# Moving the row normalisation to ScalarE and rewriting the step-size series in a ViT + Mamba + MoE kernel

## The reference, cut to what matters

```python
x = _patch_embed(images, ...)                 # 197 tokens of 128 features per image
x = _block(x, ...); x = _block(x, ...)        # 8 heads of attention, then a gated feed-forward
h = rmsnorm(x, ln_f)
...
dt = jax.nn.softplus(dt_in @ W_dt + b_dt)     # the step size of the Mamba scan, both directions
dA = jnp.exp(dt[..., None] * A)               # 16 states
dBx = dt[..., None] * Bm[:, :, None, :] * xs[..., None]
...
h = _layernorm(h + mamba_f + mamba_b)         # (x - m) / sqrt(v + eps): the "normalised rows"
h = _layernorm(h + moe(h))
```

## Time and profile before

| what | value |
|---|---|
| median of 3 runs | 8827.63 us (8824.43 to 8831.17) |
| the profiled execution's own time | 8837.69 us |
| its span, first to last instruction | 8835.9 us |
| PE, DVE, ACT busy | 80%, 80%, 70% of the span |
| POOL busy, DMA engines | 9%, about 32% |
| DVE, ACT instructions | 9195, 13424 |
| granted TensorE clock, mean | 0.918 of full speed |

### The profile page before, as it was taken

The page is one execution under the profiler, slowest core; times in us unless marked ns, Lnnn a source line. Parts: engine busy times, 40 slices in busy tenths (PEclk is TensorE's granted clock), DMA queues, the critical chain, the costliest instruction groups (busy, mean ns, idle before and its releaser), DMA issues. The chain is left out here.

```text
span 8835.9 us, 117469 instructions
## 1 busy us (share of the span) xinstructions
PE 7084.8 (80%) x33290; PEld 3962.2 (45%) x33290; DVE 7040.5 (80%) x9195; ACT 6165.8 (70%) x13424; POOL 808.2 (9%) x554
## 2 busy tenths in 40 slices
PE   6777777888888888888888888888888888888661
PEld 3444444444444444444444444444444444444330
DVE  2788888888888888888888888888888888888743
ACT  5766666677777777777777777777777777777434
POOL 0134242400000000000000000000000000000065
PEclk9998888999999999999999999999999999999775
DMA  2333323233333333333333333333333333333356
GB/s 96 110 129 115 116 100 107 102 113 118 117 118 112 117 117 116 112 121 119 118 113 116 116 118 113 117 113 120 113 116 116 117 116 116 114 120 109 129 113 199
DMA packets 282498, 1034.03 MB, mean 117 GB/s; under 512 B 37570, under 2 KB 129526, under 8 KB 273824
## 3 DMA queue, kind: packets, MB, share of 16 engines
q1 hardware_dynamic: 248352, 1009.77, 32.1%
q0 software_dynamic: 33792, 21.18, 1.5%
HBM read 951.57 MB, written 90.94 MB: 118 GB/s over the span
## 5 line engine op out<-in xcount | busy, mean ns | idle before, releaser
L1047 PE MATMUL psS<-KM,Q 128*99 128x394 f32 x4096 | 1712.5, 542 | 310.1 <-ACT PTs L578 227.6
L572 ACT ACTIVATE P<-psS,least_s 99x197 f32<-99x197 f32 x4096 | 1417.3, 434 | 640.7 <-DVE least_s L768 633.0
L843 DVE TENSOR_TENSOR_SCAN hs<-dA,hs 128x1576 f32<-128x1576 f32 x512 | 1762.1, 3442 | 62.2
L768 DVE TENSOR_REDUCE least_s<-psS 99x2 f32<-99x394 f32 x2048 | 1083.7, 560 | 312.1 <-PE psS L1047 290.2
L1054 PE MATMUL psS<-cst,P 99*99 99x99 f32 x8192 | 1077.1, 273 | 255.7 <-ACT P L572 238.6
L1054 PEld LDWEIGHTS psS<-cst,P 99*99 99x99 f32 x8192 | 931.5, 180 | 763.5 <-ACT P L572 588.2
L649 ACT ACTIVATE dA<-dt_,aneg 128x394 f32<-128x394 f32 x2048 | 1211.1, 631 | 28.2 <-DVE hs L843 19.2
L1047 PEld LDWEIGHTS psS<-KM,Q 128*99 128x99 f32 x4096 | 643.2, 178 | 1027.6 <-ACT PTs L578 501.7
L578 ACT ACTIVATE PTs<-psS 99x396 f32<-99x396 f32 x2048 | 969.0, 521 | 104.3 <-PE psS L1054 102.6
L1139 PE MATMUL psY<-hs,cst 128*128 128x394 f32 x2048 | 858.9, 551 | 136.1 <-DVE hs L852 136.1
L829 DVE TENSOR_TENSOR hs<-hs,u 128x1576 f32<-128x1576 f32 x512 | 916.3, 1790 | 52.4 <-DMA hs<-bc_scratch 52.4
(11 more groups left out here) (214 smaller groups left out, 9524.4 us busy)
## 6 DMA issues: line engine op xcount, KB each, us to landing
hs<-bc_scratch SPq DMA_DIRECT2D x512, 788.0 KB, 4.2
cr<-bc_scratch SPq DMA_DIRECT2D x512, 788.0 KB, 5.1
pat<-patches SPq DMA_DIRECT2D x64, 1176.0 KB, 7.6
more_scratch<-zeros SPq DMA_DIRECT2D x64, 197.0 KB, 5.2
rows_scratch<-hs SPq DMA_DIRECT2D x1, 12352.0 KB, 43.7
PTs<-more_scratch SPq DMA_DIRECT2D x24, 512.0 KB, 6.5
sum_scratch<-HW SPq DMA_DIRECT2D x64, 148.5 KB
hs<-rows_scratch SPq DMA_DIRECT2D x24, 386.0 KB, 3.4
```

The lines of the kernel that those rows point to most:

```text
L572: last = nc.scalar.activation(P[:, r, b, m, 0:T], psS[0:CT, 2 * r + b, m * T:(m + 1) * T], ACT.Exp, bias=least_s[:, r, b, m:m + 1], scale= ...
L768: nc.vector.tensor_reduce(least_s[:, r, b, :], psS[0:CT, 2 * r + b, 0:2 * T].rearrange("p (e t) -> p e t", e=2), axis=AX, op=ALU.min).then ...
L843: nc.vector.tensor_tensor_scan(h, a, h, 0.0, ALU.mult, ALU.add).then_inc(scan_ready, 1)
L1047: mm(psS[0:CT, 2 * r + b, 0:2 * T].rearrange("p (e t) -> p e t", e=2), Q[:, r, b, q * CT:(q + 1) * CT], KM[:, r, h % 2 * 2:h % 2 * 2 + 2, ...
```

## The change

It does four things.

1. On ACT, L639 becomes `Square` with `scale = 1/sqrt(3)` and a per-partition `bias = -sqrt(3)/4`: this gives `e^2/3 - e/2 + 3/16`. DVE adds 13/16 and multiplies by `e` in one `scalar_tensor_tensor`. The plain product of L815 is gone.
2. DVE no longer writes the rows. It forms `mrs = -mean * rstd` (99x4), and ACT writes four chunks of 99x128 as `Identity(rstd * x + mrs)` from PSUM. The waits for `rows_stored` and `slots_free` move to ACT too.
3. A constant column is added to `epsr` by POOL at the start, so `pool_ready` counts to 14. The marker semaphore `q_waited`, for which nobody waits, becomes an alias of `pool_waited`.
4. `STAGES` and `PLACE` are replaced.

```diff
-ACT_FRONT, ACT_BACK, DVE_BACK, DVE_ROUTE = (4, 5), 2, 6, 27
+ACT_FRONT, ACT_BACK, DVE_BACK, DVE_ROUTE = (4, 5), 2, 4, 27
...
-        epsr = sb("epsr", [128, 2])
+        epsr = sb("epsr", [128, 3])
...
+        mrs = sb("mrs", [CT, NC4])
...
+            nc.gpsimd.memset(epsr[:, 2:3], -(3 ** 0.5) / 4).then_inc(pool_ready, 1)
...
-                nc.scalar.activation(u[:, d, :], sp[:, :], ACT.Copy, bias=-0.5, scale=1 / 3).then_inc(poly_ready, 1)
+                nc.scalar.activation(u[:, d, :], sp[:, :], ACT.Square, bias=epsr[:, 2:3], scale=3 ** -0.5).then_inc(poly_ready, 1)
...
                 nc.scalar.activation(rstd[:, :], rstd[:, :], ACT.Exp, scale=-0.5).then_inc(rstd_ready, 1)
+                act.wait_ge(mrs_ready, i + 1)
+                act.wait_ge(rstd_ready, i + 1)
+                act.wait_ge(rows_stored, i * 32 + 16)
+                act.wait_ge(slots_free, i + 1)
+                for q in range(NC4):
+                    last = nc.scalar.activation(HW[:, q, 0:D], psY[0:CT, q * D:(q + 1) * D], ACT.Identity, bias=mrs[:, q:q + 1], scale=rstd[:, q:q + 1])
+                last.then_inc(ht_ready, 1)
...
                 dve.wait_ge(poly_ready, k)
-                back(nc.vector.tensor_tensor(u[:, d, :], u[:, d, :], sp[:, :], ALU.mult), i)
+                back(nc.vector.scalar_tensor_tensor(out=u[:, d, :], in0=u[:, d, :], scalar=13 / 16, in1=sp[:, :], op0=ALU.add, op1=ALU.mult), i)
                 dve.wait_ge(sp_ready, k)
-                back(nc.vector.scalar_tensor_tensor(out=u[:, d, :], in0=u[:, d, :], scalar=1.0, in1=sp[:, :], op0=ALU.add, op1=ALU.mult), i)
...
                 dve.wait_ge(rstd_ready, i + 1)
-                dve.wait_ge(rows_stored, i * 32 + 16)
-                dve.wait_ge(slots_free, i + 1)
-                for q in range(NC4):
-                    last = nc.vector.tensor_scalar(HW[:, q, 0:D], tokens[:, q, :], mv[:, q, 0:1], rstd[:, q:q + 1], ALU.subtract, ALU.mult)
-                last.then_inc(ht_ready, 1)
+                nc.vector.scalar_tensor_tensor(out=mrs[:, :], in0=mv[:, :, 0], scalar=-1.0, in1=rstd[:, :], op0=ALU.mult, op1=ALU.mult).then_inc(mrs_ready, 1)
```

More of the change, by code:

```diff
@@ L82, in role_stages @@
     return out
-STAGES = [('square', 1, 0), ('norm', 1, 0), ('conv', 0), ('square', 0, 0), ('qkv', 1), ('keys', 1, 0), ('norm', 0, 0), ('score', 1, 0, 0), ('score', 1, 0, 1), ('qkv', 0), ('keys', 0, 0), ('keys', 1, 1), ('turn', 1, 0, 0), ('turn', 1, 0, 1), ('score', 0, 0, 0), ('score', 1, 1, 0), ('score', 1, 1, 1), ('score', 0, 0, 1), ('turn', 1, 1, 0), ('keys', 0, 1), ('turn', 0, 0, 0), ('turn', 0, 0, 1), ('turn', 1, 1, 1), ('score', 0, 1, 0), ('score', 0, 1, 1), ('score', 1, 2, 0), ('turn', 0, 1, 0), ('score', 1, 2, 1), ('turn', 0, 1, 1), ('keys', 1, 2), ('score', 0, 2, 0), ('score', 0, 2, 1), ('turn', 1, 2, 0), ('turn', 1, 2, 1), ('keys', 0, 2), ('turn', 0, 2, 0), ('turn', 0, 2, 1), ('score', 1, 3, 0), ('score', 1, 3, 1), ('score', 0, 3, 0), ('score', 0, 3, 1), ('keys', 0, 3), ('turn', 0, 3, 0), ('turn', 0, 3, 1), ('keys', 1, 3), ('turn', 1, 3, 0), ('turn', 1, 3, 1), ('value', 0, 0), ('value', 1, 0), ('score', 1, 4, 0), ('score', 0, 4, 0), ('score', 0, 4, 1), ('score', 1, 4, 1), ('turn', 1, 4, 0), ('turn', 0, 4, 0), ('turn', 0, 4, 1), ('turn', 1, 4, 1), ('score', 1, 5, 0), ('score', 0, 5, 0), ('score', 0, 5, 1), ('score', 1, 5, 1), ('turn', 1, 5, 0), ('turn', 1, 5, 1), ('turn', 0, 5, 0), ('turn', 0, 5, 1), ('score', 1, 6, 0), ('score', 0, 6, 0), ('score', 1, 6, 1), ('score', 0, 6, 1), ('turn', 1, 6, 0), ('turn', 1, 6, 1), ('turn', 0, 6, 0), ('turn', 0, 6, 1), ('score', 1, 7, 0), ('score', 1, 7, 1), ('score', 0, 7, 0), ('score', 0, 7, 1), ('turn', 1, 7, 0), ('turn', 1, 7, 1), ('turn', 0, 7, 0), ('turn', 0, 7, 1), ('value', 1, 1), ('value', 0, 1), ('den', 1), ('den', 0), ('wo', 1), ('square', 1, 1), ('wo', 0), ('square', 0, 1), ('norm', 1, 1), ('norm', 0, 1), ('gate', 1), ('gate', 0), ('sig', 1), ('sig', 0), ('up', 1), ('up', 0), ('down', 1), ('square', 1, 2), ('norm', 1, 2), ('down', 0)]
@@ new lines @@
+STAGES = [('square', 1, 0), ('norm', 1, 0), ('conv', 0), ('square', 0, 0), ('qkv', 1), ('keys', 1, 0), ('norm', 0, 0), ('score', 1, 0, 0), ('score', 1, 0, 1), ('keys', 1, 1), ('qkv', 0), ('turn', 1, 0, 0), ('keys', 0, 0), ('turn', 1, 0, 1), ('score', 1, 1, 0), ('score', 0, 0, 0), ('score', 0, 0, 1), ('score', 1, 1, 1), ('turn', 1, 1, 0), ('turn', 1, 1, 1), ('keys', 0, 1), ('turn', 0, 0, 0), ('turn', 0, 0, 1), ('score', 0, 1, 0), ('score', 0, 1, 1), ('score', 1, 2, 0), ('turn', 0, 1, 0), ('score', 1, 2, 1), ('turn', 0, 1, 1), ('keys', 1, 2), ('score', 0, 2, 0), ('score', 0, 2, 1), ('turn', 1, 2, 0), ('turn', 1, 2, 1), ('keys', 0, 2), ('turn', 0, 2, 0), ('turn', 0, 2, 1), ('score', 1, 3, 0), ('score', 1, 3, 1), ('score', 0, 3, 0), ('score', 0, 3, 1), ('keys', 0, 3), ('turn', 0, 3, 0), ('turn', 0, 3, 1), ('keys', 1, 3), ('turn', 1, 3, 0), ('turn', 1, 3, 1), ('value', 0, 0), ('score', 0, 4, 0), ('value', 1, 0), ('score', 1, 4, 0), ('score', 0, 4, 1), ('score', 1, 4, 1), ('turn', 1, 4, 0), ('turn', 0, 4, 0), ('turn', 0, 4, 1), ('turn', 1, 4, 1), ('score', 1, 5, 0), ('score', 0, 5, 0), ('score', 0, 5, 1), ('score', 1, 5, 1), ('turn', 1, 5, 0), ('turn', 0, 5, 0), ('turn', 0, 5, 1), ('turn', 1, 5, 1), ('score', 0, 6, 0), ('score', 1, 6, 0), ('score', 0, 6, 1), ('score', 1, 6, 1), ('turn', 1, 6, 0), ('turn', 0, 6, 0), ('turn', 0, 6, 1), ('turn', 1, 6, 1), ('score', 1, 7, 0), ('score', 0, 7, 0), ('score', 1, 7, 1), ('score', 0, 7, 1), ('turn', 1, 7, 0), ('turn', 1, 7, 1), ('turn', 0, 7, 0), ('turn', 0, 7, 1), ('value', 1, 1), ('value', 0, 1), ('den', 1), ('den', 0), ('wo', 1), ('square', 1, 1), ('wo', 0), ('square', 0, 1), ('norm', 1, 1), ('norm', 0, 1), ('gate', 1), ('gate', 0), ('sig', 1), ('sig', 0), ('up', 1), ('up', 0), ('down', 1), ('square', 1, 2), ('norm', 1, 2), ('down', 0)]
@@ L242, in vit_mamba_moe @@
         names = ("open_ready loaded patches_loaded pool_ready unused_ready rows_zeroed rows_stored more_zeroed hw_ready "
-                 "q_waited ht_ready conv_done sent_all pair_free all_added fin_ready mul_done half_summed "
+                 "ht_ready conv_done sent_all pair_free all_added fin_ready mul_done half_summed "
                  "slot_ready pool_waited sent_a sent_b slots_free e_out added_a added_b ids_ready sum_ready act_setup consts_ready act_back xz_done xc_ready "
@@ L249, in vit_mamba_moe @@
                  "e2_done fin_shift fin_stats pe_waited act_read pe_read pool_read dve_read act_merge dve_merge h_kept "
-                 "u_ready xb_ready e_ready e_sig e_gated win_turned taps_ready taps_done poly_ready ").split()
+                 "u_ready xb_ready e_ready e_sig e_gated win_turned taps_ready taps_done poly_ready mrs_ready ").split()
         (open_ready, loaded, patches_loaded, pool_ready, unused_ready, rows_zeroed, rows_stored, more_zeroed,
-         hw_ready, q_waited, ht_ready, conv_done, sent_all, pair_free, all_added, fin_ready,
+         hw_ready, ht_ready, conv_done, sent_all, pair_free, all_added, fin_ready,
          mul_done, half_summed, slot_ready, pool_waited, sent_a, sent_b, slots_free, e_out, added_a, added_b, ids_ready, sum_ready, act_setup,
@@ L259, in vit_mamba_moe @@
          fin_stats, pe_waited, act_read, pe_read, pool_read, dve_read, act_merge, dve_merge, h_kept, u_ready,
-         xb_ready, e_ready, e_sig, e_gated, win_turned, taps_ready, taps_done, poly_ready) = (sem(n) for n in names)
+         xb_ready, e_ready, e_sig, e_gated, win_turned, taps_ready, taps_done, poly_ready, mrs_ready) = (sem(n) for n in names)
         pair_names = ("x_ready sq_ready ms_done rs_ready hn_ready kq_done q_ready km_ready v_done v_ready round_done max_done "
@@ L267, in vit_mamba_moe @@
         w_loaded, x_loaded = ([sem(f"{n}{b}") for b in range(EBUF)] for n in ("w_loaded", "x_loaded"))
+        q_waited = pool_waited
         b_loaded = [sem(f"b_loaded{n}") for n in range(HBUF)]
@@ L532, in _ @@
             act.wait_ge(loaded, 16 * 4)
-            act.wait_ge(pool_ready, 13)
+            act.wait_ge(pool_ready, 14)
             nc.scalar.activation(before_h[:, :], c("before"), ACT.Copy)
@@ L744, in _ @@
             nc.vector.tensor_copy(open_[:, :], c("ones")[0:1, 0:1]).then_inc(open_ready, 1)
-            dve.wait_ge(pool_ready, 13)
+            dve.wait_ge(pool_ready, 14)
             dve.wait_ge(consts_ready, 1)
```

4 lines of the change are left out of this document (2 added, 2 removed).

## The result

The changed kernel took 8624.46 us in the median of four runs (8591.66 to 8642.04), the kernel before 8826.03. The ratio is 0.9769, with a 95% interval of 0.9751 to 0.9787. Forecast were 8640 us and a range of 8545 to 8790. The profiled execution is the longest of the four, with a span of 8640.2 us. What follows compares it with the profiled execution of before, which was 196 us longer.

A forecast was written before the change was run, and what follows sets the result against it. No engine is full; turns are bound by DVE's fixed order waiting on other engines, plus a low TensorE clock. Terms of -0.60, -0.60, -1.3, -0.6, 0, +0.1 give -3.0 us a turn, times 63 -189: 8640 us, range 8545 to 8790.

The forecast's parts named there:

- The sum: All terms together: -3.0 us a turn, 126.3 to 123.3; checked against one traced turn of 123.00 us.
- Series, -0.60 and -0.60: Removing L815 on DVE wins 0.60 us a turn at dt 0 and 0.60 at dt 1.
- Merge, -1.3: Rows moved from DVE to ACT at the merge: -1.3 us a turn of DVE's 1.61, ends -0.5 and -1.6.
- The reduce inside the wait: At the merge, the reduce of score 0 4 0 fits in DVE's 2.96 us wait for PE: 0.48 us.
- ACT sets the pace: Low end of the merge term: ACT becomes the slower engine, so only -0.5 us a turn is won.
- Head, -0.6: New order at the turn's start: -0.6 us; Hn waits 0.97, score waits of 1.07 go; ends +0.97 and -0.85.
- Round 3, 0: Score 1 3 1 ahead of sum 6 on PE wins 0: input 0 hangs on half 6, sum 6, load 0.
- -1.5 if it runs at full clock: Favourable end of the round 3 term: -1.5 us a turn if sum 6 runs at full clock.
- Tail, +0.1: New order at the turn's end: output 3 fills waits for the norms, ends 0.1 us late; +0.1 a turn.
- The clock comes back: Rival: PE's wait behind dt 0 shrinks, its low clock vanishes; -4.5 us a turn, 8545 us, chance 0.15.
- the clock falls in a second place: Rival: longer PE wait in the head lowers the clock; +0.75 to +3.0 us a turn, 8875 to 9015, chance 0.08.
- Only the removed work counts: Rival: the new order brings new waits, so only -1.0 us a turn, 8765 us; chance 0.22.

The follow-up runs named there:

- u5_old_series: Changed kernel with the series of before (Copy on ACT, two DVE instructions), new lists and rows on ACT kept: 8695.98 us, ratio 0.9834.
- u4_rows_on_dve: Changed kernel with the merge's rows written by DVE as before, new lists and new series kept: 8674.52 us, ratio 0.9809.
- c4_merge: Kernel before with only the merge's row writing moved to ACT (with mrs on DVE), lists and series of before: 8839.44 us, ratio 1.0017.
- u2_sum6: Changed kernel with sum 6 ahead of score 1 3 1 on PE again: 8815.03 us, ratio 0.9964.
- f4_before_dt0: Kernel before with 9 small matmuls a turn on constants ahead of score 0 2 1, in PE's wait behind dt 0: 8785.09 us, ratio 0.9940.
- f1_round7: Changed kernel with 11 small matmuls a turn on constants at the three places of round 7 where PE waits: 8540.98 us, ratio 0.9654.
- c3_series: Kernel before with only the series changed (Square on ACT, one DVE instruction), lists and rows of before: 8668.37 us, ratio 0.9824.
- u3_merge_place: Changed kernel with score 0 4 0 behind the merge again on PE, DVE and ACT: 8647.75 us, ratio 0.9778.

## Why the prediction was right, step by step

**The sum.** -3.0 us a turn was forecast and -3.2 measured in the profile. The sign, the size and the check by the one turn of 123.00 us held. Its make-up held in three terms of six (both dt and the merge), so the close total is in good part luck: the ledger's short turn wins 5.0 us and the long one 0.4, and their mix happens to come near 3. The busy times were forecast too large as well: 150 us less on DVE came out at 111, 120 more on ACT at 88.

- *Series, -0.60 and -0.60.* Right in the ledger: 0.6 at dt 0 and 0.6 from dt 1 to the denominators. ACT's 0.09 was there too: L642 takes 0.62 us. But by itself the series is worth 155 us (u5_old_series has it at 57 in the changed kernel, near the 76 forecast). I priced the work and not what a shorter PE wait does to the clock.
- *Merge, -1.3.* Right at the place I gave: 2.1 to 3.3 in the ledger. The next reduces then take 2.55 us for four in place of 1.99, as scores come late, and 0.6 is given back by dt 1. `mrs` takes 0.16 us (0.15 forecast), DVE's wait for PE before the statistics is 2.48 in place of 2.96, and ACT, after 3.05 us of waiting (under 3 was forecast), gets `mrs` 0.44 us later and writes the rows in 1.51:

```profile
4354.41 0.30 ACT L658 ACTIVATE rstd<-mv,epsr 99x4 f32<-99x4 f32 x1 [3.05 <-DVE mv L876]
...
4355.39 1.51 ACT L665 ACTIVATE HW<-psY,mrs,rstd 99x128 f32<-99x128 f32 x4 [0.44 <-DVE mrs L880]
```

For the whole turn the term was too large: the rows on ACT are worth 35 us there (u4_rows_on_dve), 0.6 a turn. The reduce inside the wait was priced at 0.48 a turn, and undoing its place changed nothing. The end I named, ACT sets the pace, is what happens on the old lists (c4_merge).

- *Head, -0.6.* Wrong. The new wait of 0.91 us came as forecast (0.97), and the scores' wait fell from 1.07 to 0.34; the sum was 0.1. Counting exponentials and copies along ACT was too loose for a term of half a us.
- *Round 3, 0.* The step that failed most. The chain I gave was right (half 6, `sum 6`, load 0, DMA; DVE still waits for it, 1.21 us). But I took `sum 6` at the 3.00 us of the earlier trace rows and left "-1.5 if it runs at full clock" as an end. The swap itself brings the full clock, because PE works while `half 6` runs: 1.4 us in the ledger, and 172 us in u2_sum6, half of them, by the estimate there, through the clock in round 7.
- *Tail, +0.1.* Wrong in sign in the short turns: 1.7 us are won between the denominators and Hn, since `wo` runs at full clock. From Hn of norm 1 1 to the end both take 19.3 us. `wo` on PE in the two turns of the ledger, before and after:

```profile
5631.53 4.61 PE L1078 MATMUL psS<-O,wts 128*128 128x394 f32 x8 [1.94 <-DVE O L773]
```
```profile
4392.21 2.91 PE L1083 MATMUL psS<-O,wts 128*128 128x394 f32 x8 [0.90 <-DVE O L783]
```

**The rivals.** "The clock comes back" and "the clock falls in a second place" both came true, in different turns of one run. The first is the turn at 1.00 that takes 120.60 us. The second is not in the head, where I put it, but in round 7. There two decays now stand ahead of the exponentials on ACT, and DVE does four reduces ahead of the gate's product, where it did two; no run puts these back. It costs 0.7 to 4.9 us in the 30 turns it hits, by the means of the table above. A line through the 51 turns gives 0.37 us for each us of low clock there, near the 0.32 that I had read from the earlier trace rows. Behind dt 0 it is cheaper: f4_before_dt0 had 5.8 us less of it in an unrouted turn and won 1.1 us (0.19 for each). That includes what the small matmuls themselves cost, but the price seems to depend on the place. "Only the removed work counts" is out, by the size.

**Left open.** Why the same program falls into short and long turns in no fixed order was not tried; all that the trace shows is that it goes with where the earlier low stretch begins. Nor was it shown which of the three waits of round 7 matters, since all three were filled together. That the worth of the rows on ACT flips from -102 to +35 us was measured, and the pace of ACT seen on the old lists; how much of the flip is clock stays open.

## What to carry to other kernels

When several engines run at four fifths and a fixed order ties them, read the granted clock beside the timeline before pricing an order. A wait on PE costs its own length and can then halve the speed of what follows. So giving PE its ready work before a wait (u2_sum6, 2%) or even idle matmuls in it (f1_round7, 1.1%) can be worth more than the work a change removes. Price a removed instruction on the order it will run in; here one part was worth 155 us alone and 57 in company, another -102 or +35. And removing a wait that only moves, as in the head, showed no gain, however visible the wait is in the timeline.

## What the runs showed of the hardware

Turn lengths bunch. 42 of 51 unrouted turns round to 126 us before; taking 1.2 us of DVE work away put 40 of 51 at 123 and none at 125 (c3_series), and c4_merge has 45 at 126, u3_merge_place 48 at 123. This program, whose loop contains a fall of TensorE's clock, does not respond to small edits in proportion. The run-to-run spread grew as well: 8591.66 to 8642.04 us for the changed kernel, whose turns come in two kinds, against 8821.83 to 8831.17 before.
